# Row variances of the second norm: matmuls against a mean column, or ScalarE squares with the accumulator output

## The chip, the core and the metric

The kernel runs on one core of a Trainium2 chip. The metric is the device time of one execution in microseconds (us), lower is better. The engines are named as in the profile: PE is TensorE's matmul, PEld its weight load, DVE is VectorE, ACT is ScalarE, POOL is GpSimd, SP is SyncE.

## What is computed

Two graph layers over 4096 nodes with 64 features. Cut to what matters:

```
h = relu(layernorm(x))                                   # first norm
scores = (h@W)@a1 [:,None] + (ent@W)@a2 [None,:]         # 4096 x 4096
att = softmax(where(adj > 0, leaky_relu(scores), -9e15))
x = x + elu(att @ ent + h)                               # first layer
h = relu((x - mean(x)) / sqrt(var(x) + 1e-5))            # second norm
x = x + (adj == 1) @ h + h                               # second layer
```

The change touches the second norm: the variance over the 64 features of each row of x, for three quarters of the rows.

## The kernel before

**Layout.** x is held transposed: `xs[:, p]` has 128 partitions and 512 columns for each of four "pairs" p of 512-row halves (NP = 4). Partitions 0 to 63 are the features of the first half, 64 to 127 those of the second. The rows of the adjacency mask come as fp8 chunks by DMA (issued by POOL) into `am`.

**The main loop** has 160 exponentials over 128 steps n, in five blocks b (HALVES = 1, 1, 2, 2, 2: one or two halves of 512 rows). Blocks 0 and 1 are 16 steps each, blocks 2, 3 and 4 are 32 each, and jt is the step within the block. In each step DVE makes the masked score `yp` (L939, 128x1024), ACT takes its exponential in place (L683), and PE multiplies it with the entity table into `pb` (L1263, four matmuls 128x512 in fp32, which the trace shows as eight records) and, every second step, sums it with a matrix of ones (L1297). There are seven yp slots (YS = 7): DVE may write step n once the sums of step n-7 are done (`pv_done`). Every fourth step DVE also decodes a chunk (L827). PE fills in other work: `biggest` (L1066), which reads the masks of the next block, and from step 50 on `neighbours` (L1176), pieces of the second layer's product with the mask.

**The second norm of pair p = b-2** is done inside block b (b = 2, 3, 4), spread over the steps by a table FIN written by hand, which gives for each part the jt behind which (or ahead of which, on PE) it stands in the engine's own order:

```
FIN = [dict(den=2, comb=2, back=3, inv=5, bc=5, t=7, e=7, c=9, xc=8, sq=9, var=9, vs=10, hi=13, r=15, mid=15, lo=18)] + [
       dict(den=2, comb=None, back=None, inv=5, bc=4, t=8, e=7, c=8, xc=8, sq=8, var=9, vs=10, hi=12, r=14, mid=14, lo=14)] * (NP - 2)
```

The first entry holds for block 2, the second for blocks 3 and 4. Every engine has one order and waits in it, so a part that waits holds all that stands behind it on its engine. The parts in the order of the data:

- DVE `rows_on` (L878, L879) finishes xs[:, p].
- PE `centred` (xc, L1135): a matmul with the matrix that subtracts the mean, into the PSUM bank `turned`.
- ACT `squares` (sq, L612, L613): from that bank the squares into `tm` and the Relu into `ta`.
- PE `variance_again` (var, L1141, L1144): four matmuls of tm against two columns of 1/64 give the variance of each row, in the bank `rowp`; four transposes turn ta so that the rows of x are on the partitions, into `turned`.
- ACT `variances` (vs, L619): copies the 128x8 variances to `rstd`.
- POOL `deviations` (L514, L515): adds 1e-5 and raises to the power of -1/2, in place.
- ACT `normed_again` (hi, L629): eight activations 128x64 that scale each turned piece by its column of rstd, into `rs`; then ACT `highs` (L636) rounds to bf16, DVE `rests` (r, L904) takes the rest, ACT `middles` (mid, L641) rounds that, DVE `lasts` (lo, L909) takes the last part. The three bf16 parts in `h3` are what `neighbours` multiplies with.

The fourth pair (p = 3) is normed behind the loop by DVE (`rows_normed`, L888 to L896), which the change leaves alone. The first norm (`squares_first`, `variance`, `variances_first`) keeps its matmuls too.

Of the kernel before, what the change touches and what calls it, by code (L numbers as in the profile page):

```python
# [62 lines left out]
def graph_layers(nc, adj_t, xt, ent, w_t, a_cols, eye, out, N, M, D):  # L63
# [110 lines left out]
    with ctx:  # L174
# [6 lines left out]
        def sem(name):  # L181
            return ctx.enter_context(nc.semaphore(name))
# [195 lines left out]
        expm_ready = sem("expm_ready")  # L378
        c_ready = sem("c_ready")
        xc_ps = sem("xc_ps")  # L380
        sq_ready = sem("sq_ready")
        var_ps = sem("var_ps")
        relu_ready = sem("relu_ready")
        var_sb = sem("var_sb")
        rstd_ready = sem("rstd_ready")
        hh_ready = sem("hh_ready")
# [163 lines left out]
        def _(act):  # L550
# [56 lines left out]
                act.wait_ge(neg_ready, b + 1)  # L607
                sc.activation(tm[:], tm[:], ACT.Exp, scale=-1.0).then_inc(expm_ready, 1)

            def squares(b):  # L610
                act.wait_ge(xc_ps, b + 1)
                sc.activation(tm[:], turned, ACT.Square).then_inc(sq_ready, 1)  # L612
                sc.activation(ta[:], turned, ACT.Relu).then_inc(relu_ready, 1)  # L613

            def variances(b):
                act.wait_ge(var_ps, b + 1)
                if b >= 1:
                    act.wait_ge(hh_ready, b)
                sc.copy(rstd[:], rowp[:, 0:2 * SUB]).then_inc(var_sb, 1)  # L619


            def normed_again(b):
                act.wait_ge(hn_ps, b + 1)
                act.wait_ge(rstd_ready, b + 1)
                hh, at = natural(b)
                for c in range(SUB):
                    for s in range(2):
                        k = c * 2 + s
                        e = sc.activation(hh[:, s * SUB + c], turned[:, k * D:(k + 1) * D], ACT.Copy,  # L629
                                          scale=rstd[:, k:k + 1])  # L630
                e.then_inc(hh_ready, 1)

# [43 lines left out]
            for n in range(STEPS_ALL):  # L676
                b, jt = block_at(n)
                act.wait_ge(y_made, n + 1)
                m = 2 // HALVES[b]
                for r in range(m):  # L680
                    y = yp[:, n % YS, r * HALF:r * HALF + width(b)]
                    at = jt * m + r
                    e = sc.activation(y, y, ACT.Exp, bias=tbias[:, at:at + 1], scale=delta[:, 0:1])  # L683
                e.then_inc(exp_done, 1)
                for p, f in NORM.items():
                    if n == f["sq"]:
                        squares_first(p)
                    if n == f["vs"]:
                        variances_first(p)
                if n == COLS_AT[-1] + 3:  # L690
                    s_cols(range(1, NP))
                if b >= 1 and jt == 1:
                    sums_out(b - 1)
                if b >= 2:
                    f = FIN[b - 2]
                    if jt == f["back"]:
                        combined()
                    if jt == f["e"]:
                        negatives(b - 2)
                    if jt == f["sq"]:  # L700
                        squares(b - 2)
                    if jt == f["vs"]:
                        variances(b - 2)
                    if jt == f["hi"]:
                        normed_again(b - 2)
                        highs(b - 2)
                    if jt == f["mid"]:
                        middles(b - 2)
                for k, v in enumerate(VISITS):
                    if n == PIECE_AT[v + 1] - 1 + (k == 2):  # L710
                        move_out(k)
                if b + 1 < NB:
                    if b >= 1 and jt == SROWS[b] + 1:
                        s_rows(b)
                    for h in range(first[b + 1], first[b + 2]):
                        if n == VOUT[b + 1]:
                            v_rows(b + 1, h)
# [277 lines left out]
        def _(pe):  # L995
# [138 lines left out]
                pe.wait_ge(c_ready, b + 1)  # L1134
                t.matmul(turned, centre, xs[:, b], start=True, stop=True).then_inc(xc_ps, 1)  # L1135

            def variance_again(b):
                pe.wait_ge(sq_ready, b + 1)
                pe.wait_ge(relu_ready, b + 1)
                for c in range(SUB):  # L1140
                    mm = t.matmul(rowp[:, 2 * c:2 * c + 2], tm[:, c * P:(c + 1) * P], mean2, start=True, stop=True)  # L1141
                mm.then_inc(var_ps, 1)
                for c in range(SUB):
                    mm = t.transpose(turned[:, c * P:(c + 1) * P], ta[:, c * P:(c + 1) * P], eyef)  # L1144
                mm.then_inc(hn_ps, 1)
# [85 lines left out]
            for n in range(STEPS_ALL):  # L1231
                b, jt = block_at(n)
                for b2 in range(1, NB):
                    for k in range(3 if b2 == 1 else 0, NQ):
                        if SUMS[b2][k] == n:
                            biggest(b2, k)
                if b >= 2:
                    f = FIN[b - 2]
                    if jt == f["comb"]:
                        combined()  # L1240
                    if jt == f["bc"]:
                        spread(b - 2)
                    if jt == f["xc"]:
                        centred(b - 2)
                    if jt == f["var"]:
                        variance_again(b - 2)
                if b + 1 < NB:
                    if b >= 1 and jt == SROWS[b]:
                        s_rows(b)
                    for h in range(first[b + 1], first[b + 2]):  # L1250
                        if n == TURN[b + 1]:
                            turn(b + 1, h)
                        if n == VROWS[b + 1]:
                            v_rows(b + 1, h)
                pe.wait_ge(exp_done, n + 1)
                if jt == 0 and b >= 2:
                    pe.wait_ge(num_sb, 2 * (b - 1))
                final = n + 1 == start_of[b + 1]
                for s in range(2):
                    at = 2 * jt + s if single(b) else jt  # L1260
                    for d in range(0, D, 32):
                        k = s * D + d
                        t.matmul(acc2(b)[k:k + 32, :], enta[:, at, d:d + 32],  # L1263
                                 yp[:, n % YS, s * HALF:(s + 1) * HALF],
                                 start=(jt == 0), stop=final, tile_position=(0, k))
                for p, f in NORM.items():
                    if n == f["var"]:
                        variance(p)
                    if n == f["dev"]:
                        deviation(p)  # L1270
                if n in COLS_AT:
                    s_cols(1 + COLS_AT.index(n))
                for v, at in enumerate(PIECE_AT):
                    if at <= n < at + SUB:
                        neighbours(v, n - at)
                batch = 4 if n >= FOUR_FROM else 2
                if n == STEPS_ALL - 1:
                    pe.wait_ge(y_summed, 2)
                    for r in range(2):
                        for s in range(2):  # L1280
                            at = r * D + s * 32
                            mm = t.matmul(dens[at:at + 32, :], onesf[:, 0:32],
                                          yp[:, SUM_IN[r] % YS, s * HALF:(s + 1) * HALF],
                                          start=False, stop=True, tile_position=(0, at))
                    mm.then_inc(pv_done, 4)
                elif jt % batch == batch - 1 and n < STEPS_ALL - 4:
                    opens = jt == batch - 1
                    if opens:
                        if b >= 1:
                            pe.wait_ge(den_sb, 2 * b)  # L1290
                        else:
                            pe.wait_ge(h0_ready, 2)
                    for m in range(n - batch + 1, n + 1, 2):
                        for r in range(2):
                            for s in range(2):
                                at = r * D + s * 32
                                mm = t.matmul(dens[at:at + 32, :], onesf[:, 0:32],  # L1297
                                              yp[:, (m + r) % YS, s * HALF:(s + 1) * HALF],
                                              start=(opens and m + batch == n + 1), stop=(final and m + 1 == n),
                                              tile_position=(0, at))  # L1300
                        mm.then_inc(pv_done, 2)
                if jt == LONE_AT:
                    lone_rows(b)
# [59 lines left out]
```

## Time and profile before

| | us |
|---|---|
| median of 3 runs | 354.4 |
| lowest, highest | 352.23, 354.82 |
| the profiled execution's own time | 355.18 |
| its span in the trace | 353.3 |

The mean granted TensorE clock of the profiled execution is 0.984 of full speed. The profiled execution lies 0.8 us above the median, and 1.9 us of it lie outside the span. Times in the trace count from the start of the span. "Idle before" is the time that an engine stood still directly ahead of a row's first instruction, with what ended it. The start of block 2's norm (jt 8) is at about 127 us, block 3's at 191 us, block 4's at 262 us.

### The profile page before, as it was taken

Reading aid. Unit: us, or ns where it says so; the run is one execution under the profiler, and the core shown is the slowest. Engines: PE = TensorE matmul, PEld = TensorE weight load, DVE = VectorE, ACT = ScalarE, POOL = GpSimd, SP = SyncE. Lnnn points to the kernel's source line nnn. Section 1 sums busy time; section 2 is a strip of 40 time slices with the busy share of each in tenths; the row PEclk is TensorE's granted clock in tenths of the full one; section 3 lists DMA queues with packets and bytes.
Section 4 is the critical chain, followed back from the end, with each engine's and each line's share of the span. In section 5 each row is a group of like instructions: output and inputs, shape, how many; then the busy total and the mean of one; then the engine's idle time right before and its main releaser. Section 6 shows DMA issues by size and latency. Waiting matters only on the chain.

```text
span 353.3 us, 8289 instructions
## 1 busy us (share of the span) xinstructions
PE 324.3 (92%) x3647; PEld 130.9 (37%) x3647; DVE 277.9 (79%) x344; ACT 204.1 (58%) x263; POOL 77.1 (22%) x118
## 2 busy tenths in 40 slices
PE   1189987899999989999999999999999999999996
PEld 1055533333332232342333434433334333344553
DVE  0682897999999999999998789899984899455201
ACT  1021479398959789666865977385749677330000
POOL 4446159822221112013002400000007000004000
PEclk9995999999999999999999999999999999999999
DMA  7999999999999999248003950000000000000011
GB/s 145 187 106 144 114 108 108 108 106 109 108 106 108 107 109 107 23 38 83 2 2 32 91 60 2 2 3 0 2 2 2 2 2 0 2 2 4 2 61 61
DMA packets 10563, 20.83 MB, mean 59 GB/s; under 512 B 1248, under 2 KB 1312, under 8 KB 10400
## 3 DMA queue, kind: packets, MB, share of 16 engines
q0 software_dynamic: 9216, 16.78, 47.9%
q1 hardware_dynamic: 1312, 3.52, 2.6%
q8 instruction: 29, 0.48, 0.6%
q14 instruction: 6, 0.05, 0.0%
HBM read 69.58 MB, written 1.05 MB: 200 GB/s over the span
## 4 chain that ended last, share of the span: by engine, by line
PE 50%; DVE 33%; POOL 4%; DMA 4%; issue 4%; ACT 3%; SPq 1%; DVEq 0%; POOLq 0%; ACTq 0%
DVE yp L939 19%; PE pb L1263 15%; PE pb L1176 10%; PE pa L1176 8%; PE pb L1297 7%; DMA xs<-xt 4%; DVE coded L827 4%; PE pb L1023 2%; PE pa L1066 2%; POOL rstd L480 2%; POOL rstd L481 1%; POOL rstd L515 1%; DVE um L806 1%; PE pb L1197 1%; DVE gmax L799 1%
## 5 line engine op out<-in xcount | busy, mean ns | idle before, releaser
L683 ACT ACTIVATE yp<-yp,tbias,delta 128x1024 f32<-128x1024 f32 (+1 forms) x160 | 162.3, 1067 | 39.5 <-DVE yp L939 39.0
L939 DVE SCALAR_TENSOR_TENSOR yp<-s8b,t8neg,coded 128x1024 f32<-128x1024 f32 (+1 forms) x160 | 161.7, 1066 | 1.1
L1263 PE MATMUL pb<-yp,enta 128*32 128x512 f32 x1024 | 130.8, 595 | 2.7 <-ACT yp L683 2.5
L1297 PE MATMUL pb<-yp,onesf 128*32 128x512 f32 x496 | 64.5, 592 | 0.0
L1176 PE MATMUL pb<-am,h 128*32 128x512 fp8e4 x960 | 61.1, 379 | 0.0
L451 POOL DMA_DIRECT2D am<-adj_t x64 | 34.7, 552 | 103.0 <-PE pb L1176 53.5
L1263 PEld LDWEIGHTS pb<-yp,enta 128*32 128x32 f32 x1024 | 29.6, 109 | 57.7 <-issue 32.4
L1176 PEld LDWEIGHTS pb<-am,h 128*32 128x32 bf16 x960 | 27.9, 97 | 44.1 <-issue 30.0
L827 DVE TENSOR_TENSOR coded<-am,vx 128x2048 uint16<-128x2048 uint16 (+1 forms) x33 | 41.4, 1255 | 2.5 <-ACT vx L578 1.1
L1176 PE MATMUL pa<-am,h 128*32 128x512 fp8e4 x576 | 33.8, 379 | 0.2 <-DVE h L909 0.2
L514 POOL TENSOR_SCALAR rstd<-rstd 128x8 f32<-128x8 f32 x4 | 2.7, 684 | 128.9 <-ACT rstd L619 81.0
L1297 PEld LDWEIGHTS pb<-yp,onesf 128*32 128x32 f32 x496 | 15.8, 110 | 23.6 <-issue 18.0
L1066 PE MATMUL pa<-am,gtab 128*32 128x512 fp8e4 x256 | 21.3, 404 | 2.9 <-DVE gmax L800 2.3
L1176 PEld LDWEIGHTS pa<-am,h 128*32 128x32 bf16 x576 | 16.3, 97 | 20.5 <-issue 9.0
L1066 PEld LDWEIGHTS pa<-am,gtab 128*32 128x32 bf16 x256 | 6.8, 99 | 18.6 <-issue 17.2
L799 DVE TENSOR_SCALAR gmax<-pa,wk 128x1024 f32<-128x1024 int32 (+1 forms) x5 | 5.3, 1066 | 6.3 <-PE pa L1066 6.3
L523 POOL TENSOR_TENSOR am<-am,eyeb 128x512 fp8e4<-128x512 fp8e4 x8 | 9.5, 1210 | 0.0
L991 DVE SCALAR_TENSOR_TENSOR yp<-pa,xs 128x512 f32<-128x512 f32 x2 | 1.4, 693 | 10.0 <-PE pa L1176 10.0
L606 ACT ACTIVATE tm<-ta 128x512 f32<-128x512 f32 x4 | 2.5, 630 | 11.2 <-DVE ta L873 11.2
L568 ACT ACTIVATE s8b<-pa,delta 128x512 f32<-128x512 f32 x8 | 5.1, 685 | 6.6 <-PE pa L1043 6.6
L515 POOL TENSOR_TENSOR rstd<-rstd,mhalf 128x8 f32<-128x8 f32 x4 | 8.6, 2151 | 0.3
L904 DVE TENSOR_TENSOR rs<-rs,h 128x512 f32<-128x512 f32 x4 | 3.4, 860 | 6.5 <-ACT h L636 6.5
(177 smaller groups left out, 229.4 us busy)
## 6 DMA issues: line engine op xcount, KB each, us to landing
am<-adj_t POOLq DMA_DIRECT2D x64, 256.0 KB, 21.1
enta<-ent SPq DMA_DIRECT2D x1, 1040.0 KB, 8.8
xs<-xt SPq DMA_DIRECT2D x2, 512.0 KB, 11.7
out<-yp SPq DMA_DIRECT2D x4, 256.0 KB, 2.0
mats<-eye SPq DMA_DIRECT2D x1, 320.0 KB, 11.5
num<-w_t SPq DMA_DIRECT2D x1, 32.0 KB, 2.1
a_sb<-a_cols SPq DMA_DIRECT2D x1, 0.5 KB, 4.5
```

Of the source, the lines that this page charges most:

```text
L451: pool.dma_start(am[:, slot, at:at + CHUNK], adj_t[q]).then_inc(landed[landed_of(q)[0]], 16)
L480: link(g.tensor_scalar(rstd0[:, p], rstd0[:, p], 1.0, EPS, ALU.mult, ALU.add))
L515: g.tensor_tensor(rstd[:], rstd[:], mhalf[:], ALU.pow).then_inc(rstd_ready, 1)
L523: g.tensor_tensor(e, e, eyeb[:].unsqueeze(1).to_broadcast([P, SUB, P]), ALU.add, saturate=False).then_inc(own_ready, 1)
L683: e = sc.activation(y, y, ACT.Exp, bias=tbias[:, at:at + 1], scale=delta[:, 0:1])
L799: link(v.tensor_scalar(gmax[:, 0:W], sums, wk[:], None, ALU.min))
L827: return v.tensor_tensor(coded[:].bitcast(U16).rearrange("p (t i) -> p t i", t=t)[:, lo:hi], am[:, slot_of[U]].bitcast(U16).rearrange("p ( ...
L939: y = v.scalar_tensor_tensor(out=yp[:, n % YS, r * HALF:r * HALF + W], in0=s8b[:, pair(b) % 2, cols(b)], scalar=t8neg[:, at:at + 1], in1=c ...
L1066: mm = t.matmul(pa[g * KC:(g + 1) * KC, first[b] % 2 + i], gtab[:, jt], am[:, slot, at:at + HALF], start=(k == 0), stop=(k == NQ - 1), til ...
L1176: mm = t.matmul(gather(v)[at:at + 32, :], h3[:, jt, k * D + d:k * D + d + 32], masks(v, i, s), start=(v in OPENS and i == 0 and k == 0), s ...
L1263: t.matmul(acc2(b)[k:k + 32, :], enta[:, at, d:d + 32], yp[:, n % YS, s * HALF:(s + 1) * HALF], start=(jt == 0), stop=final, tile_position ...
L1297: mm = t.matmul(dens[at:at + 32, :], onesf[:, 0:32], yp[:, (m + r) % YS, s * HALF:(s + 1) * HALF], start=(opens and m + batch == n + 1), s ...
```

## The change

For the three pairs normed in the loop:

- `squares` becomes `centred_out`: ACT copies the centred bank once, unclipped, to ta (semaphore xc_sb), where it made the squares and the Relu.
- `variance_again` becomes `turned_again`: PE waits for xc_sb and does only the four transposes. The four matmuls against the mean columns and the use of `rowp` are gone.
- `variances`: ACT waits for the transposes (hn_ps) instead of the variances' matmuls (var_ps). It takes eight squares of 128x64 straight from the turned bank, with scale 64^-1/2 as an immediate and the accumulator output into one column of rstd each; the squares themselves go to tm and are not read.
- `normed_again` applies Relu in place of Copy in its eight activations, since the turned rows are no longer clipped.

FIN is unchanged, as are DVE's and POOL's orders.

```
--- before.py
+++ after.py
@@ -378,9 +378,7 @@
         expm_ready = sem("expm_ready")
         c_ready = sem("c_ready")
         xc_ps = sem("xc_ps")
-        sq_ready = sem("sq_ready")
-        var_ps = sem("var_ps")
-        relu_ready = sem("relu_ready")
+        xc_sb = sem("xc_sb")
         var_sb = sem("var_sb")
         rstd_ready = sem("rstd_ready")
         hh_ready = sem("hh_ready")
@@ -607,16 +605,18 @@
                 act.wait_ge(neg_ready, b + 1)
                 sc.activation(tm[:], tm[:], ACT.Exp, scale=-1.0).then_inc(expm_ready, 1)
 
-            def squares(b):
+            def centred_out(b):
                 act.wait_ge(xc_ps, b + 1)
-                sc.activation(tm[:], turned, ACT.Square).then_inc(sq_ready, 1)
-                sc.activation(ta[:], turned, ACT.Relu).then_inc(relu_ready, 1)
+                sc.copy(ta[:], turned).then_inc(xc_sb, 1)
 
             def variances(b):
-                act.wait_ge(var_ps, b + 1)
+                act.wait_ge(hn_ps, b + 1)
                 if b >= 1:
                     act.wait_ge(hh_ready, b)
-                sc.copy(rstd[:], rowp[:, 0:2 * SUB]).then_inc(var_sb, 1)
+                for k in range(2 * SUB):
+                    e = sc.activation(tm[:, k * D:(k + 1) * D], turned[:, k * D:(k + 1) * D], ACT.Square,
+                                      scale=D ** -0.5, accum_out=rstd[:, k:k + 1])
+                e.then_inc(var_sb, 1)
 
 
             def normed_again(b):
@@ -626,7 +626,7 @@
                 for c in range(SUB):
                     for s in range(2):
                         k = c * 2 + s
-                        e = sc.activation(hh[:, s * SUB + c], turned[:, k * D:(k + 1) * D], ACT.Copy,
+                        e = sc.activation(hh[:, s * SUB + c], turned[:, k * D:(k + 1) * D], ACT.Relu,
                                           scale=rstd[:, k:k + 1])
                 e.then_inc(hh_ready, 1)
 
@@ -698,7 +698,7 @@
                     if jt == f["e"]:
                         negatives(b - 2)
                     if jt == f["sq"]:
-                        squares(b - 2)
+                        centred_out(b - 2)
                     if jt == f["vs"]:
                         variances(b - 2)
                     if jt == f["hi"]:
@@ -1134,12 +1134,8 @@
                 pe.wait_ge(c_ready, b + 1)
                 t.matmul(turned, centre, xs[:, b], start=True, stop=True).then_inc(xc_ps, 1)
 
-            def variance_again(b):
-                pe.wait_ge(sq_ready, b + 1)
-                pe.wait_ge(relu_ready, b + 1)
-                for c in range(SUB):
-                    mm = t.matmul(rowp[:, 2 * c:2 * c + 2], tm[:, c * P:(c + 1) * P], mean2, start=True, stop=True)
-                mm.then_inc(var_ps, 1)
+            def turned_again(b):
+                pe.wait_ge(xc_sb, b + 1)
                 for c in range(SUB):
                     mm = t.transpose(turned[:, c * P:(c + 1) * P], ta[:, c * P:(c + 1) * P], eyef)
                 mm.then_inc(hn_ps, 1)
@@ -1243,7 +1239,7 @@
                     if jt == f["xc"]:
                         centred(b - 2)
                     if jt == f["var"]:
-                        variance_again(b - 2)
+                        turned_again(b - 2)
                 if b + 1 < NB:
                     if b >= 1 and jt == SROWS[b]:
                         s_rows(b)
```

On ACT, in block 3 (pair 1), L683 is the loop's exponential. Before:

```order
71 L612 ACTIVATE tm<-pa 128x512
72 L613 ACTIVATE ta<-pa 128x512
73 L683 ACTIVATE yp<-yp,tbias,delta 128x1024 x2
74 L619 COPY rstd<-pa 128x8
75 L683 ACTIVATE yp<-yp,tbias,delta 128x1024 x2
76 L629 ACTIVATE rs<-pa,rstd 128x64 x8
77 L636 CAST h<-rs 128x8x64
78 L683 ACTIVATE yp<-yp,tbias,delta 128x1024 x2
```

and after:

```order
70 L610 COPY ta<-pa 128x512
71 L683 ACTIVATE yp<-yp,tbias,delta 128x1024 x2
72 L617 ACTIVATE tm,rstd<-pa 128x64 x8
73 L683 ACTIVATE yp<-yp,tbias,delta 128x1024 x2
74 L629 ACTIVATE rs<-pa,rstd 128x64 x8
75 L636 CAST h3<-rs 128x8x64
76 L683 ACTIVATE yp<-yp,tbias,delta 128x1024 x2
```

The two passes over 512 columns are one copy, and the copy of eight columns is eight accumulating squares (L617); nothing has changed its place between the exponentials.

On PE, in block 2 (pair 0), from the centring matmul on. L1263 (L1259 after) is the product with the entity table, L1297 (L1293 after) the sums with ones, L1066 the read of the next block's masks. Before:

```order
114 L1135 MATMUL pa<-xs,mats 128x512
115 L1263 MATMUL pb<-yp,enta 32x512 x4
116 L1066 MATMUL pa<-am,gtab 32x512 x8
117 L1141 MATMUL pa<-mats,tm 128x2 x4
118 L1144 MATMUL pa<-mats,ta 128x128 x4
119 L1263 MATMUL pb<-yp,enta 32x512 x4
```

and after:

```order
114 L1135 MATMUL pa<-xs,mats 128x512
115 L1259 MATMUL pb<-yp,enta 32x512 x4
116 L1066 MATMUL pa<-am,gtab 32x512 x8
117 L1140 MATMUL pa<-mats,ta 128x128 x4
118 L1259 MATMUL pb<-yp,enta 32x512 x4
```

The four matmuls of two columns are gone, and the transposes stand in their place.

## Rows read from the trace of the kernel before

**Rows 1.** The page's part 1: busy us, share of the span, instructions

```profile
PE 324.3 (92%) x3647; PEld 130.9 (37%) x3647; DVE 277.9 (79%) x344; ACT 204.1 (58%) x263; POOL 77.1 (22%) x118
```

**Rows 2.** Windows: PE, PEld, DVE, ACT, POOL busy us, PEclk, DMA share, GB/s

```profile
190.00:308.00 118.00, 117.78 (x1388) 44.87 (x1382) 101.73 (x98) 80.28 (x93) 13.43 (x14) 1.00 0.14 15
```

**Rows 3.** The chain that ended last, block 2: start us, us, what

```profile
126.88 1.12 PE pa L1135 x2
...
129.43 1.00 PE pa L1141 x8
...
130.45 0.17 ACT rstd L619
...
130.71 1.15 POOL rstd L514
...
131.94 2.59 POOL rstd L515
...
134.61 1.75 ACT rs L629 x8
...
137.65 3.67 DVE yp L939 x3
```

**Rows 4.** Timeline of block 2's norm: start us, us, what, forms, idle before

```profile
128.04 0.60 ACT L612 ACTIVATE tm<-pa 128x512 f32<-128x512 f32 x1 [1.27 <-PE pa L1135]
128.54 0.59 ACT L613 ACTIVATE ta<-pa 128x512 f32<-128x512 f32 x1
129.01 1.24 ACT L683 ACTIVATE yp<-yp,tbias,delta 128x1024 f32<-128x1024 f32 x1
129.36 0.97 PEld L1141 LDWEIGHTS pa<-mats,tm 128*128 128x128 f32 x8 [0.42 <-issue]
130.17 0.51 PEld L1144 LDWEIGHTS pa<-mats,ta 128*128 128x128 f32 x4
130.28 0.63 PE L1144 MATMUL pa<-mats,ta 128*128 128x128 f32 x4
...
137.04 0.69 DVE L904 TENSOR_TENSOR rs<-rs,h 128x512 f32<-128x512 f32 x1 [0.40 <-ACT h L636]
```

**Rows 5.** Timeline of block 3's norm, ACT and PEld

```profile
193.22 2.37 ACT L683 ACTIVATE yp<-yp,tbias,delta 128x1024 f32<-128x1024 f32 x2
195.49 0.16 ACT L619 COPY rstd<-pa 128x8 f32<-128x8 f32 x1
...
198.83 1.74 ACT L629 ACTIVATE rs<-pa,rstd 128x64 f32<-128x64 f32 x8 [0.35 <-POOL rstd L515]
...
202.42 0.13 PEld L1263 LDWEIGHTS pb<-yp,enta 128*32 128x32 f32 x4 [0.33 <-ACT yp L683]
```

**Rows 6.** Timeline of block 4's norm, ACT, DVE and PEld

```profile
264.56 2.37 ACT L683 ACTIVATE yp<-yp,tbias,delta 128x1024 f32<-128x1024 f32 x2
266.83 0.15 ACT L619 COPY rstd<-pa 128x8 f32<-128x8 f32 x1
...
270.01 1.74 ACT L629 ACTIVATE rs<-pa,rstd 128x64 f32<-128x64 f32 x8 [0.76 <-POOL rstd L515]
...
275.23 0.69 DVE L909 TENSOR_TENSOR h<-rs,h 128x512 bf16<-128x512 f32 x1 [1.55 <-ACT h L641]
...
281.03 0.38 PEld L1263 LDWEIGHTS pb<-yp,enta 128*32 128x32 f32 x8 [0.48 <-ACT yp L683]
```

**Rows 7.** Small ACT instructions: the timeline's first, then durations of L629

```profile
7.14 0.21 ACT L554 COPY num<-pa 128x64 f32<-128x64 f32 x1 [5.13 <-PE pa L1000]
7.25 0.18 ACT L555 ACTIVATE w1c<-pa 128x1 f32<-128x1 f32 x1
...
L629 ACT ACTIVATE rs<-pa,rstd x24: 306/326/358, 134.6 to 271.4; 128x64 f32<-128x64 f32 x24
```

**Rows 8.** Waits from 137 to 191 us, DVE's two: us in total, times, longest

```profile
DVE ta L878 <- ACT tm L608: 1.4, 1, 1.4
...
DVE rs L904 <- ACT h L636: 0.4, 1, 0.4
```

More of the change, by code:

```diff
@@ L380, in graph_layers @@
         xc_ps = sem("xc_ps")
-        sq_ready = sem("sq_ready")
-        var_ps = sem("var_ps")
-        relu_ready = sem("relu_ready")
+        xc_sb = sem("xc_sb")
         var_sb = sem("var_sb")
@@ L608, in negatives, with centred_out @@
                 sc.activation(tm[:], tm[:], ACT.Exp, scale=-1.0).then_inc(expm_ready, 1)
-            def squares(b):
+            def centred_out(b):
                 act.wait_ge(xc_ps, b + 1)
-                sc.activation(tm[:], turned, ACT.Square).then_inc(sq_ready, 1)
-                sc.activation(ta[:], turned, ACT.Relu).then_inc(relu_ready, 1)
+                sc.copy(ta[:], turned).then_inc(xc_sb, 1)
             def variances(b):
-                act.wait_ge(var_ps, b + 1)
+                act.wait_ge(hn_ps, b + 1)
                 if b >= 1:
                     act.wait_ge(hh_ready, b)
-                sc.copy(rstd[:], rowp[:, 0:2 * SUB]).then_inc(var_sb, 1)
+                for k in range(2 * SUB):
+                    e = sc.activation(tm[:, k * D:(k + 1) * D], turned[:, k * D:(k + 1) * D], ACT.Square,
+                                      scale=D ** -0.5, accum_out=rstd[:, k:k + 1])
+                e.then_inc(var_sb, 1)
             def normed_again(b):
@@ L628, in normed_again @@
                         k = c * 2 + s
-                        e = sc.activation(hh[:, s * SUB + c], turned[:, k * D:(k + 1) * D], ACT.Copy,
+                        e = sc.activation(hh[:, s * SUB + c], turned[:, k * D:(k + 1) * D], ACT.Relu,
                                           scale=rstd[:, k:k + 1])
@@ L700, in _ @@
                     if jt == f["sq"]:
-                        squares(b - 2)
+                        centred_out(b - 2)
                     if jt == f["vs"]:
@@ L1135, in centred, with turned_again @@
                 t.matmul(turned, centre, xs[:, b], start=True, stop=True).then_inc(xc_ps, 1)
[L1137 to L1142, printed above, removed]
+            def turned_again(b):
+                pe.wait_ge(xc_sb, b + 1)
                 for c in range(SUB):
@@ L1245, in _ @@
                     if jt == f["var"]:
-                        variance_again(b - 2)
+                        turned_again(b - 2)
                 if b + 1 < NB:
```

## The prediction

> **What bounds the kernel.** I read the busy shares first. PE is busy 92% of the span, DVE 79%, ACT only 58% [rows 1]. That says little by itself, because an engine with spare time can still be waited for. So the second view is the busy time by stretch: from 190 to 308 us PE is busy 117.78 of 118.00 us, at the full granted clock of 1.00 (2.4 GHz) [rows 2]. There PE is the bound, and it is so from block 3's norm on. The third view is the chain that ended last. In block 2 it does not run along PE. It runs once through the whole norm: centring matmul, variance matmuls, ACT's copy, POOL's two operations, ACT's eight scalings, the rounding, and then DVE, which goes on with its scores [rows 3]. So of the three places that the change touches, one (block 2) has the norm's latency itself as the bound, and two (blocks 3 and 4) lie where PE is full. The fourth view, the timeline, shows how much room there is. In block 2 DVE stands 0.40 us waiting for the rounded rows (L904) [rows 4]. In block 3 PE waits 0.33 us for the exponential of step 13, which stands on ACT behind the norm's scalings [rows 5]. In block 4 it waits 0.48 us for that of step 16, and DVE has waited 1.55 us ahead of it for ACT [rows 6]. In all three places somebody already waits for the ACT work that lies behind the norm. Whatever delays that work delays the kernel, and PE time that is saved ahead of such a wait only makes the wait longer.
>
> **The change, part by part.** I call S the time from the start of the first accumulating square to the end of the last write of rstd.
>
> PE loses the four matmuls against the mean columns, 1.00 us in the chain of block 2 [rows 3] and about as much in the two other blocks. The transposes come 0.81 us earlier: their first weight load stood at 130.17, that of the removed matmuls at 129.36 [rows 4]. They take from 130.17 to the end at 130.91 (130.28 + 0.63), 0.74 us. So in block 2 they end at 129.36 + 0.74 = 130.10.
>
> ACT's pass at sq becomes one copy for two activations. The next instruction started 0.97 us after the first of the two (128.04 to 129.01), and 0.50 after it where one pass of the same size follows the other (128.04 to 128.54) [rows 4]. So ACT is 0.47 us earlier at its next exponential. The copy, started at 128.04, ends by 128.64, ahead of the 129.36 at which PE comes to the transposes: the new wait on xc_sb costs nothing in block 2, and by the same distance nothing in the others.
>
> The eight squares are the cost. The trace of before has no accumulating activation, so S is bounded. From below: a 128x64 copy from PSUM is followed by the next instruction 0.11 us later (7.14 to 7.25) [rows 7]. If the accumulator output were free, S would be 8 x 0.11 = 0.88 us. From above: if the accumulator must be written by a step of its own, and neither overlaps the other, a pair costs 0.21 for the 64 columns and 0.18 for one column [rows 7], 0.39 us, S = 3.1. With the longest row for this shape, L629 at 0.326 us with its pointer scale, in place of the 0.21 it would be 0.51, S = 4.0 [rows 7]. Between lies the group of the same shape in a row of eight, L629: 1.75 us for eight, 0.22 each [rows 3]. I take 0.32 us a square, S = 2.56. That is nearer to the unoverlapped pair than to L629, because the sum can only be given out when its last column has been added, and the next square can't begin to add before that.
>
> Two rules of the Trainium skill bear on this price. A pass over 512 columns is followed by the next after 0.50 us [rows 4], and one over 64 columns after 0.11 us [rows 7]. The page "ScalarE: Activation LUTs" of the Trainium skill (What ACT_TABLE_LOAD costs) gives 186 ns plus 0.833 ns a column with immediates, less an overlap of 93 ns: an estimated 0.52 and 0.15 us, near the rows. If the accumulator output adds nothing to that, S is an estimated 1.2 us and the sum below would be +1.8. The page "VectorE: DVE Perf Modes" of the Trainium skill (Two Vector instructions with no wait between them) states that on VectorE an operation which also writes out its accumulator is two instructions, the main one and an accumulator read. If ScalarE does likewise, a square is an estimated 0.24 us by the first page, S 1.9 and the sum +4.0. The trace of before shows neither.
>
> Now the three places. **Block 2.** The squares can start at 130.10 + 0.04 = 130.14, when the transposes are done: ACT's exponential ahead of them ends at 129.01 - 0.47 + 1.24 = 129.78. POOL starts 0.10 us behind the last write, as it did before (130.45 + 0.17 = 130.62, POOL at 130.71) [rows 3]. So POOL starts at 130.24 + S instead of 130.71: later by S - 0.47 = 2.1 us. POOL, the scalings and the rounding follow unchanged, and ACT is not late for them: its three exponentials between take as long as before and shift by about as much. DVE already waits 0.40 us at L904, so all 2.1 us land on it. From there to block 3's norm DVE waits only once more, 1.4 us for the exponential L608 of the next pair, whose input DVE itself has just made [rows 8]: that wait moves along with it. So nothing gives the 2.1 us back.
>
> **Block 3.** Here ACT's own order decides the start: the two exponentials end at 193.22 + 2.37 - 0.47 = 195.12, and the transposes are done long before. With the usual overlap of 0.1 us the squares start at 195.0. POOL starts at 195.1 + S instead of about 195.74 (195.49 + 0.16 and 0.09 on) [rows 5]: later by S - 0.64 = 1.9 us. The scalings, the rounding and the exponential of step 13 go with it. PE comes to step 13 about 1 us earlier and leaves it 1.9 us later, since it waited 0.33 us already [rows 5]. The saved microsecond is spent waiting.
>
> **Block 4.** The same by the same rows: the squares start at 264.56 + 2.37 - 0.47 - 0.1 = 266.36, POOL at 266.46 + S instead of 267.08 (266.83 + 0.15 and 0.10 on) [rows 6], later by S - 0.62 = 1.9 us. The delay goes through L641, L909 (where DVE waits 1.55 us), DVE's next score and ACT's exponential to step 16, where PE waits 0.48 us already [rows 6].
>
> The sum is 3S - 1.73 = 7.68 - 1.73 = +5.95 us. From 308 us on nothing is changed. Against the profiled execution that is 355.2 + 5.9 = 361.1 us. The profiled run lay 0.8 us above the median, so against the median it is 354.4 + 5.95 = 360.4 us, 1.7% slower.
>
> Relu in place of Copy in L629 is the same instruction with another function: nothing, as L612 and L613 with Square and Relu take 0.60 and 0.59 us [rows 4].
>
> **The rivals.** (1) *The accumulator output is nearly free.* At 0.11 us a square S is 0.88 and the sum 3 x 0.88 - 1.73 = +0.9 us, 355.3 us: no change. For it speaks that plain passes overlap so well [rows 7]. Against it, that the sum of a row must be complete before it is written. (2) *PE's gain counts and ACT's delay is covered by the seven yp slots.* In blocks 3 and 4 PE is full [rows 2], so each removes 1.0 us; with block 2 at +2.1 that is about +0.1, and 354.5 us. With S at 1.9, as well, block 2 costs 1.4 and the kernel becomes 0.6 us faster, 353.8. Faster by more than 1% it can hardly be: all of PE's savings together are 3 us, 0.8%. Against it speak the two waits of PE for an exponential right behind the norm [rows 5, 6]: the slots are empty there. (3) *The squares cost as two full instructions, the long form.* S = 4.0, sum +10.3, 364.7 us. (4) *POOL's two operations take another time than before*, once they no longer fall beside the same DVE work. In block 2 they took 3.7 us [rows 3]. A change of half a microsecond in one block goes onto the end in full, either way, and widens the range by about 1 us.
>
> **How the numbers follow.** The forecast, S between 2 and 3.2, has a chance of 0.62, with a range of its own from 358.7 to 362.3 us. Rival 1, with all S under 2, has 0.15, rival 2 0.11, rival 3 with all S above 3.2 0.12. About 1% (3.5 us) is what a measurement of this kernel can tell from no change. The sum passes it at S = 1.75, 0.22 us a square. So slower by over 1% has 0.62 + 0.12 and a third of rival 1's 0.15, in all about 0.78. Faster by over 1% needs more than all of PE's savings and gets 0.03. The rest, 0.19, is no change. The range from 355.3 to 364.3 us reaches to rival 1's end and nearly to rival 3's.
>
> **What would show it.** Right: L617 and its accumulator steps take some 2.6 us in each of three places, PE's 24 records of L1141 are gone, DVE's wait at `rests` in block 2 grows from 0.40 to about 2.5 us, and PE waits about 3 us for the exponential of step 13 in block 3 and 1 to 3 us at steps 13 to 16 of block 4. POOL's start in block 2 moves from 130.7 to about 132.8 us. Wrong: squares that follow each other in under 0.2 us; PE waits in blocks 3 and 4 that stay under 0.5 us, which would mean that the slots cover the delay; or a DVE wait at `rests` of block 2 that grows while the later steps catch up before 190 us.

## The result and the profile after

The changed kernel takes 357.4 us (median of 4 runs) against 353.5 us of before measured beside it: ratio 1.0097, 95% interval 1.0056 to 1.0138. The medians lie 3.9 us apart; the ratio, which is used below, makes it some 3.4 us. The forecast was 360.4 us, +5.95 us. The direction was right, the size was not.

The timed sets spread by 2.6 us (before) and 2.0 us (after) from run to run. The traces show where: the first centring matmul of block 2, which the change leaves alone up to there, starts at 126.88 us in the trace of before, at 126.51 in that of after, and between 124.22 and 127.18 in all twelve traces of this study, with the granted clock of the first 40 us between 0.87 and 1.00. So the traces are compared by stage: from the centring matmul of block 2 to that of block 3, to that of block 4, and to the last sum with ones behind the loop. These are the four rows of the chain that ended last in the trace after (start us, us, what):

```profile
126.51 1.13 PE pa L1135 x2
...
191.78 1.14 PE pa L1135 x2
...
264.02 1.07 PE pa L1135 x2
...
309.61 0.86 PE pb L1278 x8
```

In the trace of before the same rows are:

```profile
191.09 1.13 PE pa L1135 x2
...
262.50 1.06 PE pa L1135 x2
...
308.12 0.86 PE pb L1282 x8
```

with the first, 126.88, in [rows 3]. The three stages last 64.21, 71.41 and 45.62 us before and 65.27, 72.24 and 45.59 after: +1.06, +0.83 and -0.03, together **+1.9 us** in the loop. Behind the last sum 45.2 us remain in all twelve traces. So by the traces what the 3.4 us have beyond the 1.9 lies ahead of block 2's norm, where the start differs by up to 3 us from trace to trace. It is no later in the two traces of after (126.51 and 124.93) than in that of before. That and the repeated runs below speak for the spread and against a cost of the change outside the loop; the timed figures alone can't tell.

The eight squares are sixteen rows on ACT. The first two pairs of block 2, and the exponentials behind the last (timeline: start us, us, what, idle before):

```profile
127.67 0.59 ACT L610 COPY ta<-pa 128x512 f32<-128x512 f32 x1 [1.27 <-PE pa L1135]
128.15 1.24 ACT L683 ACTIVATE yp<-yp,tbias,delta 128x1024 f32<-128x1024 f32 x1
129.68 0.22 ACT L617 ACTIVATE tm<-pa 128x64 f32<-128x64 f32 x1 [0.29 <-PE pa L1140]
129.80 0.19 ACT L617 ACTIVATION_READ_ACCUMULATOR tm<-pa 128x1 f32 x1
129.90 0.21 ACT L617 ACTIVATE tm<-pa 128x64 f32<-128x64 f32 x1
130.00 0.20 ACT L617 ACTIVATION_READ_ACCUMULATOR tm<-pa 128x1 f32 x1
...
131.27 3.54 ACT L683 ACTIVATE yp<-yp,tbias,delta 128x1024 f32<-128x1024 f32 x3
```

An accumulating square is two instructions, and the pairs follow each other every 0.195 us (129.90 to 130.09 and so on), not every 0.32. The chain of block 2 shows what S became, and what lies behind it:

```profile
129.06 0.60 PE pa L1140 x4
...
129.68 1.76 ACT tm L617 x16
131.44 0.08 issue
131.52 1.16 POOL rstd L512
...
132.76 2.59 POOL rstd L513
...
135.43 1.76 ACT rs L629 x8
```

S is 1.76 us, where the forecast had 2.56. POOL starts 5.01 us behind the centring matmul (126.51), where it started 3.83 behind it [rows 3]: +1.18. Everything behind it in this block has its old length. DVE's wait at `rests` is 1.59 us where it was 0.40, +1.19 (timeline):

```profile
137.86 0.69 DVE L904 TENSOR_TENSOR rs<-rs,h 128x512 f32<-128x512 f32 x1 [1.59 <-ACT h L636]
```

In blocks 3 and 4 the waits named in the prediction grew, at the places named (timeline, PEld; block 3's step 13, block 4's steps 15 and 16):

```profile
204.31 0.16 PEld L1259 LDWEIGHTS pb<-yp,enta 128*32 128x32 f32 x8 [2.42 <-ACT yp L683]
```

```profile
280.17 0.16 PEld L1259 LDWEIGHTS pb<-yp,enta 128*32 128x32 f32 x8 [0.30 <-ACT yp L683]
...
282.75 0.16 PEld L1259 LDWEIGHTS pb<-yp,enta 128*32 128x32 f32 x8 [1.56 <-ACT yp L683]
```

They answer to the 0.33 us of [rows 5] and the 0.48 us of [rows 6]. The row of PE itself stood still for less, and ahead of the same instructions in the trace of before not at all (timeline, PE):

```profile
204.31 1.07 PE L1259 MATMUL pb<-yp,enta 128*32 128x512 f32 x8 [1.51 <-ACT yp L683]
...
282.75 1.07 PE L1259 MATMUL pb<-yp,enta 128*32 128x512 f32 x8 [0.65 <-ACT yp L683]
```

### The profile page after: what moved, and what is told of

Same layout as the page of the kernel before. It is cut to its first block, busy times and chain, and to the rows that moved or that the text cites. A ratio compares the mean times of both kernels' runs of the same rounds, so it can differ in the third digit from the quotient of the medians.

```text
span 354.8 us, 8280 instructions
## 1 busy us (share of the span) xinstructions
PE 324.3 (91%) x3623; PEld 128.1 (36%) x3623; DVE 277.6 (78%) x344; ACT 206.6 (58%) x305; POOL 76.4 (22%) x118
## 4 chain that ended last, share of the span: by engine, by line
PE 47%; DVE 29%; ACT 9%; POOL 5%; DMA 4%; issue 4%; SPq 1%; DVEq 0%; ACTq 0%; POOLq 0%
DVE yp L939 16%; PE pb L1259 14%; PE pb L1172 9%; PE pb L1293 7%; PE pa L1172 6%; DMA xs<-xt 4%; ACT yp L683 4%; DVE coded L827 4%; POOL rstd L513 2%; PE pa L1066 2%; ACT rs L629 1%; POOL rstd L478 1%; ACT tm L617 1%; PE pa L1013 1%; DVE gmax L799 1%
## 5 line engine op out<-in xcount | busy, mean ns | idle before, releaser
L683 ACT ACTIVATE yp<-yp,tbias,delta 128x1024 f32<-128x1024 f32 (+1 forms) x160 | 162.0, 1068 | 37.5 <-DVE yp L939 37.1
L1259 PE MATMUL pb<-yp,enta 128*32 128x512 f32 x1024 | 133.2, 603 | 5.8 <-ACT yp L683 5.6
L1293 PE MATMUL pb<-yp,onesf 128*32 128x512 f32 x496 | 65.9, 604 | 0.0
L1259 PEld LDWEIGHTS pb<-yp,enta 128*32 128x32 f32 x1024 | 29.3, 110 | 63.3 <-issue 30.6
L1293 PEld LDWEIGHTS pb<-yp,onesf 128*32 128x32 f32 x496 | 16.0, 111 | 24.2 <-issue 18.6
L1066 PE MATMUL pa<-am,gtab 128*32 128x512 fp8e4 x256 | 20.9, 395 | 2.3 <-DVE gmax L800 2.3
L1066 PEld LDWEIGHTS pa<-am,gtab 128*32 128x32 bf16 x256 | 6.8, 97 | 17.5 <-issue 16.4
L991 DVE SCALAR_TENSOR_TENSOR yp<-pb,xs 128x512 f32<-128x512 f32 x2 | 1.4, 692 | 9.0 <-PE pb L1172 9.0
```

What stands on the lines that cost most here:

```text
L1066: mm = t.matmul(pa[g * KC:(g + 1) * KC, first[b] % 2 + i], gtab[:, jt], am[:, slot, at:at + HALF], start=(k == 0), stop=(k == NQ - 1), til ...
L1259: t.matmul(acc2(b)[k:k + 32, :], enta[:, at, d:d + 32], yp[:, n % YS, s * HALF:(s + 1) * HALF], start=(jt == 0), stop=final, tile_position ...
L1293: mm = t.matmul(dens[at:at + 32, :], onesf[:, 0:32], yp[:, (m + r) % YS, s * HALF:(s + 1) * HALF], start=(opens and m + batch == n + 1), s ...
```

## The experiments

Each kernel was timed beside before on the same chip. The table gives each trace by stage, as differences to the trace of before, in us; the expectations and verdicts follow.

| kernel | block 2's stage | block 3's | block 4's | sum | timed ratio, 95% interval |
|---|---|---|---|---|---|
| after | +1.06 | +0.83 | -0.03 | +1.9 | 1.0097 (1.0056 to 1.0138) |
| after again | +1.08 | +0.84 | -0.02 | +1.9 | 1.0068 (1.0037 to 1.0099) |
| squares twice | +2.27 | +2.62 | +1.61 | +6.5 | 1.0214 (1.0161 to 1.0267) |
| squares without sums | -0.13 | +0.83 | -0.24 | +0.5 | 0.9999 (0.9967 to 1.0030) |
| four idle matmuls on PE | +1.07 | +0.84 | -0.03 | +1.9 | 1.0047 (1.0015 to 1.0079) |
| change in block 2 only | +2.56, of it 1.50 in a stretch of lower clock | 0.00 | 0.00 | +1.1 without that | 1.0051 (1.0015 to 1.0086) |
| after, table later | +0.35 | -0.89 | -0.90 | -1.4 | 0.9968 (0.9938 to 0.9998) |
| the same again | +0.36 | -0.89 | -0.90 | -1.4 | 0.9993 (0.9963 to 1.0023) |
| before, table later | 0.00 | 0.00 | 0.00 | 0.0 | 0.9995 (0.9958 to 1.0032) |
| after, squares at step 9 | +0.34 | +0.83 | -0.22 | +1.0 | 1.0031 (1.0001 to 1.0061) |
| blocks 3 and 4, table later | 0.00 | -0.89 | -0.89 | -1.8 | 0.9996 (0.9965 to 1.0027) |

The stages repeat to 0.02 us between two traces of one kernel, while the timed ratios carry about 0.3 to 0.4% each way. Where a verdict is finer than that, it rests on the stages.

**The squares twice.**

```
-                for k in range(2 * SUB):
-                    e = sc.activation(tm[:, k * D:(k + 1) * D], turned[...], ACT.Square,
-                                      scale=D ** -0.5, accum_out=rstd[:, k:k + 1])
+                for r in range(2):
+                    for k in range(2 * SUB):
+                        e = sc.activation((num, tm)[r][:, k * D:(k + 1) * D], turned[...], ACT.Square,
+                                          scale=D ** -0.5, accum_out=(spare, rstd)[r][:, k:k + 1])
```

> The kernel after, with the eight accumulating squares taken twice (the first eight write num and a spare tile, which nobody reads then). In the trace of after the eight pairs follow each other at 0.195 us, 1.56 us for eight. Theory A (what stands on ACT ahead of var_sb lands on the end in full in all three blocks): 3 x 1.56 = +4.7 us over after, +8.1 over before (ratio about 1.023 to before). Theory B (in blocks 3 and 4 the slots of yp cover the squares, only block 2 pays): +1.6 us over after, +5.0 over before (1.014).

Measured: 1.0214, and +4.6 us over after by the stages, against 4.7 of theory A and 1.6 of theory B. The timed interval, 1.0161 to 1.0267, leaves theory B's 1.014 out. What stands on ACT ahead of rstd goes onto the end in all three blocks; the slots of yp do not cover it. But the blocks pay +1.21, +1.79 and +1.64 us over after, not 1.56 each, so that the sum comes so near is in part luck. They follow the end of POOL's second operation, which comes 1.20, 1.79 and 1.63 us later than in after, counted from the centring matmul.

**Squares without the accumulator output.** This kernel leaves the variances out: rstd holds squares of eight of the turned values.

```
-                    e = sc.activation(tm[...], turned[...], ACT.Square, scale=D ** -0.5, accum_out=rstd[:, k:k + 1])
-                e.then_inc(var_sb, 1)
+                    sc.activation(tm[...], turned[...], ACT.Square, scale=D ** -0.5)
+                sc.activation(rstd[:], turned[:, 0:2 * SUB], ACT.Square).then_inc(var_sb, 1)
```

> The kernel after with eight squares without the accumulator output, and one square of eight columns into rstd in their place (the variances are left out, so the output differs). A square of 64 columns should follow the next at 0.11 us, so the stretch ahead of var_sb falls from 1.75 to about 8 x 0.11 + 0.17 = 1.05 us. Theory A: 3 x 0.70 = -2.1 us against after, +1.3 us against before (1.004). Theory B: -0.7 us against after, +2.7 over before (1.008). If the squares cost the same 0.2 us without the accumulator, the time is that of after.

Its timeline in block 2:

```profile
127.39 1.04 ACT L617 ACTIVATE tm<-pa 128x64 f32<-128x64 f32 x8 [0.29 <-PE pa L1140]
128.23 0.27 ACT L619 ACTIVATE rstd<-pa 128x8 f32<-128x8 f32 x1
```

Eight squares take 0.84 us to the next start, 0.105 each: the accumulator read costs the other 0.09 us of a pair. The stretch ahead of var_sb is the 1.1 us that was expected. The sum of the stages is 1.4 us under after, between the two theories (2.1 and 0.7), and block 3 did not gain at all: +0.83, as in after. The reason stands in POOL's rows. Block 3, here and in after:

```profile
193.38 1.09 POOL L512 TENSOR_SCALAR rstd<-rstd 128x8 f32<-128x8 f32 x1 [4.28 <-ACT rstd L619]
194.55 2.59 POOL L513 TENSOR_TENSOR rstd<-rstd,mhalf 128x8 f32<-128x8 f32 x1
```

```profile
197.52 0.43 POOL L512 TENSOR_SCALAR rstd<-rstd 128x8 f32<-128x8 f32 x1 [4.93 <-ACT tm L617]
198.03 2.59 POOL L513 TENSOR_TENSOR rstd<-rstd,mhalf 128x8 f32<-128x8 f32 x1
```

From block 3's centring matmul (188.30 and 191.78) POOL starts at 5.08 and 5.74 us, but its second operation starts at 6.25 in both. The first took 1.09 us instead of 0.43. DVE's rows in the kernel without sums tell what it ended with:

```profile
193.13 2.48 DVE L939 SCALAR_TENSOR_TENSOR yp<-s8b,t8neg,coded 128x1024 f32<-128x1024 f32 x2
```

The first of these two scores ends 1.28 us from the start, at 194.41, and POOL's operation at 194.47. In block 2 of after it is the same: POOL starts at 131.52 and ends 0.05 us behind a score of DVE. There the earlier start did pay: 4.37 us behind the centring matmul in place of 5.01, it fell under the score before, and POOL's second operation ended 1.20 us earlier, by the length of one score; the stage is 1.19 us shorter.

**Four matmuls given back to PE, read by nobody.**

```
                 mm.then_inc(hn_ps, 1)
+                for c in range(SUB):
+                    t.matmul(rowp[:, 2 * c:2 * c + 2], ta[:, c * P:(c + 1) * P], mean2, start=True, stop=True)
```

> The kernel after with four matmuls of 128x2 put back on PE behind the transposes, on the copied rows, into the old bank; nobody reads them. PE is given back the 1.0 us in each block without touching the chain of the norm. Theory A (in blocks 3 and 4 PE waits for an exponential behind the norm anyway): block 2 nothing, block 3 nothing (it waits 1.5 us or more there), block 4 nothing to 0.6 us; in all +0 to +0.6 us over after. Rival (PE is full, the saved matmuls count): +2.0 us over after, +5.4 over before (1.015).

The stages are those of after to 0.01 us. With this table PE's saving is worth nothing: PE's idle time ahead of step 13 falls from 1.51 to 0.72 us and ahead of step 16 from 0.65 to 0. The rival's +2.0 us falls. (The timed ratio is 1.0047 where after had 1.0097, with the same loop: so far apart can two such figures lie.)

**The change in block 2 alone.** Pair 0 as in after, pairs 1 and 2 as before.

> The change in block 2 alone (pair 0); blocks 3 and 4 keep squares, Relu and the variance matmuls. Theory A: S - 0.47 = 1.75 - 0.47 = +1.3 us over before (1.0036). Rival (the loss comes from blocks 3 and 4, or from the early part of the program): 0.

Blocks 3 and 4 are at 0.00. Block 2's stage is 2.56 us longer, but this execution had a stretch of lower granted clock in it, which the others had not in the loop (windows; PE, PEld, DVE, ACT, POOL busy us, PEclk, DMA share, GB/s):

```profile
135.00:140.00 5.00, 3.56 (x37) 0.67 (x29) 3.41 (x4) 4.71 (x12) 0.17 (x1) 1.00 1.06 108
140.00:145.00 5.00, 5.00 (x32) 1.40 (x36) 4.96 (x5) 5.00 (x5) 0.00 (x0) 0.66 0.64 64
```

At the exponentials of steps 46 and 48, ahead of that stretch, the delay is 1.20 us, as in after. The stage of after ends with 1.06 us, this one with 1.50 more, all of it gathered in the stretch. That the clock did it is read from the one coincidence. With 1.1 to 1.2 us theory A's 1.3 holds; the timed interval, 1.0015 to 1.0086, holds its 1.0036 and leaves the rival's 1 out.

**The change once more.**

> The kernel after once more, to size the change itself. In its first trace PE's delay grows by 1.9 us between step 40 and the end of the loop (1.07 in block 2, 0.83 in block 3, 0 in block 4), and the first 40 us, which the change leaves alone, differ from run to run by up to 2.6 us. Theory A (the loop's 1.9 us are all, the 3.4 us of the first comparison contain the start's spread): ratio about 1.0054. Rival (the change really costs 3.4 us or more, part of it outside the loop): 1.0097.

Its stages are those of the first trace to 0.02 us. The ratio, 1.0068, lies between theory A and the rival, and its interval, 1.0037 to 1.0099, holds the values of both. So the timing doesn't decide between them; the stages do for the loop, where the change is worth +1.9 us. The timed figure is 0.5 us higher here, which the start's spread leaves open.

**The parts behind rstd one step later, on after and on before.**

```
-    FIN = [dict(..., vs=10, hi=13, r=15, mid=15, lo=18)] + [
-           dict(..., vs=10, hi=12, r=14, mid=14, lo=14)] * (NP - 2)
+    FIN = [dict(..., vs=10, hi=14, r=16, mid=16, lo=18)] + [
+           dict(..., vs=10, hi=13, r=15, mid=15, lo=16)] * (NP - 2)
```

> The kernel after with the parts behind rstd one step later in the table: block 2 hi 14, r 16, mid 16 (lo stays 18), blocks 3 and 4 hi 13, r 15, mid 15, lo 16. Theory A: the later variances are waited for by nobody, so block 2 costs +0.2 us against before instead of +1.1, and in blocks 3 and 4 PE's saved 1.0 us each now counts: about -1.8 us against before (0.995). Rival (the order was already the best, another wait takes the place): the time of after or more.

> The kernel before with the same later entries of the table: the control for the run on the shifted kernel after. Theory A: block 2 gains at most DVE's 0.40 us, blocks 3 and 4 nothing, since PE is full there and its matmuls remain: -0.4 to 0 us (0.999 to 1.000). Rival (the gain of the shifted kernel comes from the table alone): about -1.8 us.

> The shifted kernel after once more, beside the run with the change in blocks 3 and 4 alone: -1.4 us between step 40 and the end of the loop, ratio 0.996, as in its first run. If the ratio of that run (0.9968) held a lucky start, this one lies nearer 1.

Behind block 2 PE now gains 0.89 us in each block, near the 1.00 us of the matmuls in [rows 3], and block 2 costs 0.35 us in place of 1.06. Together that is -1.4 us, where theory A had -1.8: each block came out 0.10 to 0.15 us worse than expected. On before the same table changes nothing, 0.00 in every stage: the gain is that of the change once nobody waits for the norm. The wait of step 13 is gone, and from block 3's centring matmul to the last sum the chain that ended last holds nothing but PE's rows, of which these set the stages:

```profile
189.65 1.13 PE pa L1135 x2
...
260.17 1.05 PE pa L1135 x2
...
304.89 0.86 PE pb L1278 x8
```

This kernel is faster than after (0.9968 and 0.9993 against 1.0068 and 1.0097, with intervals that don't meet). Against before it is 1.4 us better in the loop; of the two timed ratios the first is just clear of 1 and the second, nearer to 1, is not.

**The squares one step earlier.** Block 2 as in the shifted kernel; blocks 3 and 4 `vs=9, hi=12, r=14, mid=15, lo=16`.

> The kernel after with block 2 as in the shifted kernel, and in blocks 3 and 4 the squares one step earlier (vs 9) with hi 12, r 14, mid 15, lo 16. ACT then waits for the transposes up to 0.7 us at vs, and the squares start 0.5 us earlier. Theory A: POOL starts 0.5 us earlier than in after, but the exponential of step 13 still stands behind the scalings, so blocks 3 and 4 gain less than in the shifted kernel: -0.5 to -1.0 us against before (0.998).

Wrong: +1.0 us in place of -0.5 to -1.0. Block 3 costs the same 0.83 as in after, although POOL begins 0.5 us earlier:

```profile
196.24 0.93 POOL L512 TENSOR_SCALAR rstd<-rstd 128x8 f32<-128x8 f32 x1 [4.43 <-ACT tm L617]
197.25 2.59 POOL L513 TENSOR_TENSOR rstd<-rstd,mhalf 128x8 f32<-128x8 f32 x1
```

Counted from its centring matmul at 191.00 POOL starts at 5.24 us and its second operation again at 6.25: the half microsecond went into the first operation. With hi at 12, step 13's exponential is as late as ever. So in block 3 the place of hi decides, with r behind it, and not that of the squares. Block 4 says something else. There nothing waits behind hi any more, and what is lost against the later table (-0.22 in place of -0.90) is lost at step 10: its exponential now stands behind the squares, and PE waits for it. The chain that ended last in block 4, and PE's row in the timeline:

```profile
266.56 1.75 ACT tm L617 x16
268.31 1.14 ACT yp L683
```

```profile
269.49 1.06 PE L1259 MATMUL pb<-yp,enta 128*32 128x512 f32 x8 [0.46 <-ACT yp L683]
```

Both blocks lose 0.67 us there; in block 3 the wait of step 13 comes on top and hides it.

**The change in blocks 3 and 4 alone, with the later table.**

> The change in blocks 3 and 4 alone, with the later table of the two shifted kernels; block 2 keeps squares, Relu and the variance matmuls. In the traces block 2 of the shifted kernel before adds 0.0 us and blocks 3 and 4 of the shifted kernel after take 0.89 us each off PE. Theory A (where PE is the bound and nobody waits for the norm, the change is worth its matmuls; where the norm's latency is the bound it only costs): -1.8 us between step 40 and the end of the loop, ratio 0.995. Rival (block 2's change is needed for what follows, or the gain is no sum of the blocks): -1.4 us or less.

By the stages 0.00, -0.89 and -0.89: the blocks add up, and this is the best loop of all, 1.8 us under before. The timed ratio of 0.9996 doesn't show it; its interval, 0.9965 to 1.0027, neither holds the expected 0.995 nor tells this kernel from before. So the 1.8 us are shown in the loop of one trace, and whether they reach the time of an average run stays open. The profiled execution took 353.24 us against the 355.18 of before, with nearly the same start (the centring matmul at 126.80 and 126.88 us).

## Why the prediction was right and wrong

**What bounds the kernel: right.** Block 2 is bound by the norm's latency, blocks 3 and 4 by PE with a wait right behind the norm. The waits grew where they were said to, but by less: DVE's at `rests` to 1.59 us and not 2.5, PE's own at step 13 to 1.51 and not 3. PE's saving was spent in them (the run with four idle matmuls).

**The price of a square: the step that failed.** The term was S = 2.56 us from 0.32 us a square; it measured 1.76 us, 0.195 a square. By the prediction's own sum, 3S - 1.73, that is +3.5 instead of +5.95, so this term alone holds 2.4 of the 4.1 us by which the loop's +1.9 was missed. That +3.5 is also near the timed 3.4 us is luck, since only 1.9 of these lie in the loop. The squares follow each other in under 0.2 us, one of the prediction's own signs of being wrong. Its argument was that the sum can only be given out when the last column is added, and that the next square can't begin to add before. The rows show no such wait: the read starts 0.10 us behind the start of its square, whose own row lasts 0.22, and the next square starts 0.10 behind that. The durations overlap as those of plain small instructions do: a plain square is 0.105, near the 0.11 of the small copy in [rows 7], and a read adds the start-to-start distance of one more small instruction, not its duration. Taken by start-to-start distances, the rows would have given 2 x 0.11 = 0.22. The upper end of S was misread as well: 0.326 us is the median of L629 in [rows 7] and 0.358 the longest, which makes it 4.3 and not 4.0. The rule of the page "VectorE: DVE Perf Modes" in the Trainium skill, two instructions where the accumulator is written out, holds on ScalarE as well; the estimate made with it and with "ScalarE: Activation LUTs", 0.24 us a square, was nearer than mine.

**"POOL follows unchanged": wrong in block 4.** POOL began 1.09 us later there, counted from the centring matmul (269.69 - 264.02 against 267.08 - 262.50), close to the prediction's S - 0.62 = 1.14. Its end came only 0.19 later. These are its rows before, and after:

```profile
267.08 1.10 POOL L514 TENSOR_SCALAR rstd<-rstd 128x8 f32<-128x8 f32 x1 [64.49 <-ACT rstd L619]
268.26 1.66 POOL L515 TENSOR_TENSOR rstd<-rstd,mhalf 128x8 f32<-128x8 f32 x1
```

```profile
269.69 0.20 POOL L512 TENSOR_SCALAR rstd<-rstd 128x8 f32<-128x8 f32 x1 [67.30 <-ACT tm L617]
269.97 1.66 POOL L513 TENSOR_TENSOR rstd<-rstd,mhalf 128x8 f32<-128x8 f32 x1
```

By 269.69 DVE had finished its last score and stood waiting, so the operation took 0.20 us in place of 1.10. That is 0.9 us of the miss, and it is rival 4, which had been given half a microsecond. In the run with the later table a score starts there at the end of the first operation, and POOL's pair takes 0.20 and 2.71 us.

In blocks 2 and 3 the sum missed something too, which its numbers hide. It let the end move with S, microsecond for microsecond, but POOL's end moves in steps of what DVE does. Its second operation ends 7.64 and 7.65 us behind the centring matmul before and 8.83 and 8.84 after, 1.19 us later in both, and one score of DVE follows the other after 1.20 us. In block 3 it ends at 8.84 also where POOL starts 0.5 or 0.7 us earlier (squares at step 9, squares without sums). That the starts of after, 1.18 and 1.09 us later than before, lie near the 1.19 is no proof of the sum.

**"PE waits already 0.33 and 0.48 us": misread.** Those are waits of the weight loads. PE's matmuls still ran on from the queue, as [rows 2] had said: 117.78 busy of 118.00 us. So the first part of the delay was hidden in blocks 3 and 4. In block 3 the weight load of step 13 came 1.20 us later, and of step 14 only 0.83. In block 4 step 16 came 0.20 us later (counted from step 104), the end of the loop 0.03 earlier. In block 2 0.12 of the 1.20 us were made up by step 52, for another reason, which was not followed up. Together 0.7 us. A weight load's wait is a wait of PE only where PE's own row is idle too.

With 2.4, 0.9 and 0.7 us the +5.95 come down to +1.95, against the loop's measured +1.9.

**The rivals.** The free accumulator (S = 0.88) is out by 0.9 us of S, yet the run without sums shows what even it would have given: +0.5 us, no gain. That the slots of yp cover the delay fell with the squares taken twice; that PE's gain counts came true only with the later table. POOL's other time, rival 4, came true in block 4; it had a width and no chance of its own. The long form fell by the rows. The chances (0.78 for slower by over 1%) leaned too far: the ratio of 1.0097 lies at that bound, and the loop's +1.9 us is 0.5%, inside no change.

## What to carry to other kernels

Price a series of small instructions by the distance from start to start of neighbours in the trace, not by their durations; that includes the accumulator read. When work moves from a full engine onto the path that this engine waits for, ask first who waits behind it: here the saving of 0.9 us a block appeared only when the parts behind it stood one step later in the table. Move one part at a time: the run with the squares earlier moved a wait to step 10 and put back that of step 13, and only the chain told them apart. And count a wait of PEld as PE's only where PE is idle in the same moment.

## What the runs showed of the hardware

ScalarE's accumulator output is a second instruction, ACTIVATION_READ_ACCUMULATOR, at 0.09 us from start to start in a row of eight.

POOL's small operations depend on what DVE does beside them. The 128x8 tensor_scalar takes 0.20 us where DVE is idle, and otherwise, in 41 of the 48 of the twelve traces, ends 0.05 to 0.06 us behind the DVE instruction under way at its start, up to 1.16 us after its own start. The power of 128x8 takes 1.66 us beside an idle DVE. With a score under way at its start it takes 2.58 to 2.71, and in all 27 such cases it ends 1.52 to 1.53 us behind the end of that score. A score that starts later leaves it alone, as block 4 of before with the later table shows:

```profile
266.45 1.66 POOL L515 TENSOR_TENSOR rstd<-rstd,mhalf 128x8 f32<-128x8 f32 x1
```

```profile
267.44 1.28 DVE L939 SCALAR_TENSOR_TENSOR yp<-s8b,t8neg,coded 128x1024 f32<-128x1024 f32 x1 [1.13 <-PE pb L1297]
```

So POOL's part of such a chain is stepped: a start 0.5 to 0.7 us earlier brought nothing in block 3 of two runs, and 0.64 us earlier brought 1.20 in block 2 of one. This agrees with the page "SBUF — State Buffer" of the Trainium skill (Who interferes with whom), which states that a VectorE instruction with two inputs in SBUF contends with a GpSimd instruction that reads SBUF; the score has two such inputs. No run here took one of those inputs away, so the cause is that page's, and only the coincidence in time is shown.
